# Hybrid layer on one core: the scan's broadcast rows issued by ACT in place of SP, with a new order of the main passes

## What is computed

```python
ssm = einsum('bti,si->bts', xc, W_x)          # 16 states, of each a row B and a row C
Bp, Cp = ssm[..., :16], ssm[..., 16:]
dt = softplus(einsum('bti,oi->bto', xc, W_dt) + b_dt)
def step(h, inp):
    x_t, b_t, c_t, dt_t = inp
    dA = exp(dt_t[..., None] * A)
    h = dA * h + dt_t[..., None] * b_t[:, None, :] * x_t[..., None]
    return h, einsum('bds,bs->bd', h, c_t)
```

## Time and profile before

| | |
|---|---|
| time, median of 3 runs | 3764.75 us (3763.28 to 3771.59) |
| the profiled execution | 3763.91 us, its span 3761.8 us |
| PE, ACT, DVE, POOL busy | 90%, 85%, 71%, 36% |
| DMA engines busy with the program's transfers | 47.4% |
| length of one pass of MAIN | 217.5 us |

### The profile page before, as it was taken

The page is one execution under the profiler, slowest core; times in us unless marked ns, Lnnn a source line. Parts: engine busy times, 40 slices in busy tenths (PEclk is TensorE's granted clock), DMA queues, the critical chain, the costliest instruction groups (busy, mean ns, idle before and its releaser), DMA issues. The chain is left out here.

```text
span 3761.8 us, 38380 instructions
## 1 busy us (share of the span) xinstructions
PE 3394.5 (90%) x11446; PEld 1446.9 (38%) x11446; DVE 2664.6 (71%) x3513; ACT 3199.0 (85%) x4034; POOL 1341.8 (36%) x758
## 2 busy tenths in 40 slices
PE   3896899999999999999999999999999999998847
PEld 1231334434343444434344443434344443434424
DVE  3537868687776868677686867778686877769582
ACT  2787899898999999899998989999998999886643
POOL 2112324344343434434342433424243443314251
PEclk9896899999999999999999999999999999999978
DMA  5324345455544545454454545454454645435332
GB/s 156 112 82 116 126 137 174 141 179 148 164 149 138 170 131 185 146 167 142 155 171 135 177 132 185 143 159 159 139 181 125 187 145 164 149 107 171 111 136 76
DMA packets 214847, 552.01 MB, mean 147 GB/s; under 512 B 25105, under 2 KB 96626, under 8 KB 214642
## 3 DMA queue, kind: packets, MB, share of 16 engines
q1 hardware_dynamic: 214642, 549.57, 47.4%
HBM read 488.65 MB, written 63.18 MB: 147 GB/s over the span
## 5 line engine op out<-in xcount | busy, mean ns | idle before, releaser
L785 PE MATMUL bank<-hF,wst 128*128 128x512 f32 x2304 | 1146.3, 619 | 29.7 <-ACT hF L887 15.2
L1332 POOL TENSOR_TENSOR yM<-yM,ws 128x1024 f32<-128x1024 f32 x240 | 630.6, 2628 | 1399.8 <-DVE ws L1231 1396.8
L1112 DVE TENSOR_TENSOR rPool<-bank,rPool 128x512 f32<-128x512 f32 x1024 | 700.5, 686 | 525.4 <-PE bank L713 411.5
L887 ACT ACTIVATE hF<-bank,cols 128x512 f32<-128x512 f32 x1152 | 771.6, 687 | 248.8 <-PE bank L774 233.6
L1025 ACT ACT_TABLE_LOAD x528 | 677.4, 1283 | 9.3
L887 ACT ACTIVATE rPool<-bank 128x512 f32<-128x512 f32 x1024 | 572.0, 597 | 92.5 <-PE bank L708 84.8
L772 PE MATMUL bank<-xnH,wst 128*128 128x512 f32 x1152 | 605.0, 525 | 30.3 <-ACT hF L887 18.3
L1224 DVE TENSOR_TENSOR_SCAN ws<-dAs,ws 128x1024 f32<-128x1024 f32 x256 | 598.7, 2345 | 7.2 <-ACT dAs L887 0.8
L785 PEld LDWEIGHTS bank<-hF,wst 128*128 128x128 f32 x2304 | 419.0, 193 | 464.2 <-issue 366.0
L713 PE MATMUL bank<-qpk,kpk 48*128 48x512 bf16 x1024 | 406.0, 398 | 97.8 <-DVE rPool L1112 93.6
L887 ACT ACTIVATE rPool<-rPool 128x2048 f32<-128x2048 f32 x256 | 490.5, 1916 | 2.1
(11 more groups left out here) (157 smaller groups left out, 2951.6 us busy)
## 6 DMA issues: line engine op xcount, KB each, us to landing
wst<-wscr SPq DMA_DIRECT2D x288, 768.0 KB, 5.9
bc<-bcscr SPq DMA_DIRECT2D x256, 512.0 KB, 4.6
cB<-gscr SPq DMA_DIRECT2D x256, 256.0 KB, 4.7
qscr<-parts SPq DMA_DIRECT2D x192, 128.0 KB, 2.4
kscr<-parts SPq DMA_DIRECT2D x192, 128.0 KB, 2.1
kpk<-kscr SPq DMA_DIRECT2D x128, 192.0 KB, 5.3
qpk<-qscr SPq DMA_DIRECT2D x128, 192.0 KB, 5.7
wscr<-wst SPq DMA_DIRECT2D x9, 512.0 KB, 5.5
```

What stands on the lines that cost most here:

```text
L785: pe.matmul(ps[FFN][:, :], w2, hF[:, (NCH * f + q) % HSLOTS, :], start=(c == 0), stop=(c == FC - 1)).then_inc(s_dn, 1)
L887: return nc.scalar.activation(out_, in_, fn, **kw)
L1112: v.tensor_tensor(rP[:, slot, c, :], ps[num_bank(b, s)][:, :], rP[:, slot, c, :], ALU.mult).then_inc(s_mul, 1)
L1332: g.tensor_tensor(yM[:, :, :], yM[:, :, :], ws[:, s % 3, :, :], ALU.add).then_inc(s_ya, 1)
```

## The change

`bc` leaves SP's order and enters ACT's. The code of the step stays the same apart from SP's `settled`, an increment of a semaphore that nobody waits for. In SECOND and LAST the orders of PE, DVE and POOL stay as they were, and ACT's is the old one with the `bc` steps put in; in MAIN the orders of all five engines are new. The number of steps of every kind stays the same on PE, DVE and POOL, and on ACT but for `bc`.

```diff
@@ SP, scan @@
                     sp.dma_start(bcscr[m].rearrange("s u t -> (s u) t"), rowBC[:, :]).then_inc(s_bcst, 16)
-                elif name == "bc":
-                    sp.wait_ge(s_bcst, floor(16 * (m + 1)))
-                    settled(sp)
-                    sp.wait_ge(s_hc, floor(NS * m + s - 1))
-                    settled(sp)
-                    src = bcscr[m][s:s + 1].rearrange("s u t -> s (u t)").broadcast_to([P, 2 * 512])
-                    sp.dma_start(bc[:, s % 2, :, :].rearrange("p u t -> p (u t)"), src).then_inc(s_bc[s % 2], 16)
@@ ACT @@
+            def rows_in(m, s):
+                act.wait_ge(s_bcst, floor(16 * (m + 1)))
+                act.wait_ge(s_hc, floor(NS * m + s - 1))
+                src = bcscr[m][s:s + 1].rearrange("s u t -> s (u t)").broadcast_to([P, 2 * 512])
+                nc.scalar.dma_start(bc[:, s % 2, :, :].rearrange("p u t -> p (u t)"), src).then_inc(s_bc[s % 2], 16)
+
...
-                    if kind == "M":
+                    if kind in ("M", "N") and name == "bc":
+                        rows_in(i - 1 if kind == "M" else i - 2, n)
+                    elif kind == "M":
                         scan(i - 1, name, n)
-                    if kind == "N":
+                    elif kind == "N":
                         decay(i - 2, n)
@@ MAIN, ACT: one line of the table, as an example @@
-    T.gelu H.gelu*2 T.log A.ln*4 N.decay A.ex T.gelu H.gelu*2 F.mean H.gelu*6 T.log A.ln N.decay A.ln*2 F.var A.ln*2
+    T.gelu H.gelu*2 T.log A.ln*2 N.decay N.bc A.ln*2 A.ex T.gelu H.gelu*2 N.bc F.mean H.gelu*6 T.log A.ln*2
```

More of the change, by code:

```diff
@@ L90 @@
     "SP": """
-    P.in F.w*3 F.rows F.gate F.w*2 F.gate*3 F.w F.gate F.w*3 F.gate*3 A.load M.rows M.bc*2 P.pk*2 A.load M.bc*2
-    P.pk*2 P.ahead M.bc*3 P.ahead
+    P.in F.w*3 F.rows F.gate F.w*2 F.gate*3 F.w F.gate F.w*3 F.gate*3 A.load M.rows P.pk*2 A.load P.pk*2 P.ahead*2
 """,
@@ L132 @@
 """,
     "PE": """
[L134 to L147, removed]
+    H.down*3 A.den*2 H.up A.den*2 A.num H.up H.down A.v F.mean H.down A.num H.down H.up*2 A.num H.up*4 A.num A.den*2
@@ L148 @@
+    A.num A.den*2 G.down*2 A.num*2 A.av A.num G.up*2 G.down*2 G.up*3 A.den*2 A.num*2 A.den A.num G.down A.av G.up
+    A.num G.down*2 G.up*2 A.num G.down A.den A.num A.den G.up A.num A.den*3 G.down A.num G.down A.den*2 G.up A.den
+    A.num A.av A.num*2 G.down*2 A.num*2 G.up*2 A.num*2 A.av*2 G.up*2 A.close
 """,
     "ACT": """
-    T.gelu H.gelu*2 T.log A.ln*4 N.decay A.ex T.gelu H.gelu*2 F.mean H.gelu*6 T.log A.ln N.decay A.ln*2 F.var A.ln*2
-    A.ex N.decay T.gelu H.gelu*2 T.log A.ln F.router N.decay T.gelu F.gelu*4 T.log A.ln*2 H.close P.load A.ln*2 A.ex
@@ L152 @@
[L152 to L156, removed]
@@ new lines @@
+    H.close A.ln P.load A.ex N.bc A.ln*2 P.mean A.ln*2 P.var N.decay*2 T.gelu F.gelu N.bc F.gelu*5 T.log A.ln*2 A.ex
+    P.qk A.ln*2 N.bc P.qk A.ex N.decay N.bc T.gelu F.gelu*6 T.log A.ln*4 P.qk A.ex N.decay A.ln*5 N.bc A.ex N.decay
+    T.gelu F.gelu*8 T.log A.ln*2 P.cast P.qk T.gelu F.gelu P.cast F.gelu*2 T.log A.ln E.mean A.ex A.ln*3 E.var A.ln
+    T.gelu F.gelu*3 P.cast F.gelu*2 T.log A.ex A.ln*2 G.mean G.var T.gelu F.gelu*4 P.cast T.log A.ln*2 G.router
+    P.cast T.gelu G.gelu*5 M.mean T.log M.var A.ex M.xp A.ln*2 M.xp T.gelu G.gelu*2 M.xp G.gelu*2 T.silu M.silu M.xp
@@ L170 @@
+    E.var E.gate F.part G.mean A.mul*2 F.part G.var A.mul G.router G.route F.part G.turn M.mean A.mul M.var A.mul*2
+    M.conv*8 A.mul*6 G.part A.mul M.dt M.dbx*2 M.scan M.hc A.mul G.part A.mul M.scan A.mul*2 M.dbx M.scan M.hc
+    G.part M.hc A.mul*4 M.dbx*2 A.mul M.scan A.mul*2 G.part A.mul M.scan M.hc A.mul*3 M.hc A.mul*2 G.part A.mul*3
+    M.dbx*2 M.scan*2 A.close M.hc*2
 """,
     "POOL": """
-    H.add N.acc*2 H.add*3 N.acc*5 F.add P.rope F.add N.acc*2 P.rest F.add*2 P.rest*2 P.rope P.rest F.add*3 M.take
```

66 lines of the change are left out of this document (37 added, 29 removed).

## The result

The changed kernel takes 3922.19 us (median of 4 runs, 3912.44 to 3923.45) where the kernel before takes 3768.17 on the same chip. The ratio is 1.0409, 95% interval 1.039 to 1.0428. It is 4.1% slower; the forecast was 0.4% slower, and the range ended at 3826 us. The profiled run took 3912.44 us, its span is 3910.4 us, 148.6 longer than that of before.

A forecast was written before the change was run, and what follows sets the result against it. The prediction took the PE-ACT round, with DVE third, to bound the kernel, not one engine. 13 x (0 + 0.5 - 0.3 + 0.7) = 11.7 us plus 3 for the end, on 3763.91, gave about 3778 us; range 3718 to 3826.

The forecast's parts named there:

- Issuing on ACT: ACT's queue: 256 `bc` issues of 0.32 us are paid beside running activations; nothing taken, 82 us the upper end.
- Waiting on ACT: ACT's sequencer, held until `hc` is ready, queues later instructions late: 0.5 us a pass taken, 1.8 at most.
- Given back by the transfers: DVE's waits for `bc` and PE's for expert weights shrink with a freer SP queue: -0.3 us a pass.
- The new order of PE: PE in MAIN: adjacent `A.num` pairs go from 2 to 7, costing 0.7 us a pass of a possible 4.3.
- the 10.8 us that it waits inside the runs: ACT's waits for `up` in a pass of MAIN, 139.9 us in 13 passes, would not shrink much.
- The end: LAST: `bc` issued late by ACT delays the finish by 0 to 6.7 us; 3 taken.
- The expectation of under 15: Sign in LAST: DVE's wait for `bc`, 14.7 us before, stays under 15 us.
- ACT paying in full: Rival: ACT's queue cannot hide issues and waits; 3830 us, ends 3800 and 3869, chance 0.07.
- The better order: Rival: the new MAIN order shortens PE's waits at the score products; 3735 us, chance 0.34.
- no change: Rival: issues and transfers are hidden and the new order equals the old; 3764 us, 3757 to 3771, chance 0.23.
- PE's wait at L713's counterpart grows from 3.6 us a pass: Sign in MAIN: PE waits longer for the numerators' bank at a score product than 3.6 us a pass.

The follow-up runs named there:

- issues_on_act: Kernel before, SP still issuing `bc`, plus 256 small transfers issued by ACT without a real wait: 3773.44 us, ratio 1.0032.
- waits_on_act: Kernel before, SP still issuing `bc`, with ACT only waiting for the same semaphores where it would issue `bc`: 3781.64 us, ratio 1.0050.
- sp_new_order: Kernel before, SP still issuing `bc`, with MAIN's new order on all five engines: 3919.73 us, ratio 1.0412.
- pairs_old: Kernel before, SP issuing `bc`, only PE's MAIN order edited to have the new order's adjacent `A.num` pairs: ratio 1.0128.
- the halves: Kernel before, SP issuing `bc`, MAIN's new order only up to `G.mean`: ratio 1.0259; only from there: 1.0472; only from behind `M.mean`: 1.0200.
- new_unpaired: sp_new_order with PE's adjacent `A.num` pairs parted down to two: ratio 1.0321 to the kernel before.
- run 14: Not a follow-up run: the words belong to the sentence that MAIN is run 14 times in the kernel, so no change or time of its own.
- act_old_order: Kernel before with `bc` issued by ACT, but MAIN's old order kept on every engine: 3809.96 us, ratio 1.0138.

## Why the prediction was wrong

- **Issuing on ACT, taken as nothing.** Right in mechanism. 256 issues cost 12 us by issues_on_act, not 82, and in the new order nothing that can be seen. Of the 84 us that ACT's issues last in the changed kernel, 74 lie beside running activations or table loads.
- **Waiting on ACT, 13 x 0.5 = 6.5 us.** Too small in the old order: 19 us (waits_on_act, 12 to 26) against a bound of 23. By which path they come is open, since PE stood still no longer there. In the new order, for which the term was meant, waits and issues together cost nothing that can be measured.
- **Given back by the transfers, -0.3 a pass.** The waits went the other way. DVE waits 28.0 us for rows in place of 5.9, PE for weights 2.8 in place of 1.4. Against sp_new_order the freer SP did serve the weights earlier (2.8 us for 7.2), but the rows, at their places on ACT, came later (28.0 us for none), and neither shows in the time.
- **The new order of PE, +0.7 a pass.** This is the step that failed. Measured: 145 us in 13 passes, 11.2 a pass, with the rows still issued by SP. The argument for a sixth of the pairs' price was that they "lie in a stretch where PE is hardly idle", from which it took them to be covered. It is the other way round: where PE is hardly idle, nothing covers a new wait. At full price the pairs would have been 4.3 us; pairs_old measured 3.6. The other 7 us or so had no term at all. The prediction asked of the new order only what it did to pairs, and not what else it moved on PE; the halves and new_unpaired (8.8 us a pass with two pairs, as before) show that this was the larger part. Nor had it a term for matmuls that take longer, 3.9 us of PE's busy time a pass. MAIN is also run 14 times and not 13, which by the prediction's own terms is 0.9 us.
- **"ACT's order has the same table loads and runs of `gelu`, so the 10.8 us that it waits inside the runs have no reason to shrink much."** They grew: 139.9 to 237.2 us, since ACT waits for PE's `up`. ACT's idle time in a pass, foreseen to grow by 1 us, went from 18.3 to 28.1. What matters is how one order lies to the other, and the sameness of one says nothing.
- **The end, +3.** Right in size: DVE's wait for rows in LAST rose from 14.7 to 19.6 us, 4.9 more, and the part behind MAIN grew by 5.5. The expectation of under 15 was missed.
- **Rivals.** ACT paying in full is refuted by issues_on_act, and with real transfers by act_old_order, 50 us in all and not 105. ACT's busy time, 200.19 us a pass for 199.18, which was to show it, can't: issues aren't counted in it. The prediction had said that a pass of 221 us or more would mean this rival; the pass is 228.3, and it means the order. A rule that reads one number for one cause was too short. The better order and no change are refuted by sp_new_order. The range left out a worse order altogether, though its other side, a better order by 29 us, was priced.
- **"PE's wait at L713's counterpart grows from 3.6 us a pass":** it did, to 8.2.

What stays open: which moved steps make the 7 to 9 us a pass that are not pairs. Most of them arise before `G.mean`, where the new order has only one pair more: 7.7 - 1.2 = 6.5 us there, against 5.5 behind `M.mean` with four pairs more, which at 3.6 / 5 = 0.7 us each leave about 5.8 and 2.6. No experiment went to single steps there.

## What to carry to other kernels

When two engines hand work to and fro below a microsecond, a rewritten order can be the largest part of a change, and not a side effect of it. Test it apart from the change, and price each new back-to-back use of a single buffer in full where the waiting engine has no slack. An engine that computes nothing is a good place for a transfer that must wait for a buffer, however long it stands there; on a computing engine the issue is nearly free, and the wait in front of it is not, and a place a few instructions too early can cost more than one that is too late.

## What the runs showed of the hardware

- A transfer issued by ACT takes 0.326 us on its queue, where SP took 0.320. 256 small ones of 0.33 us, issued by ACT with no wait, made the kernel only 12 us longer, some 0.05 us each.
- A wait on ACT ahead of such an issue holds up what stands behind it: ACT stood for 5.73 us with a table load behind a `bc` whose buffer wasn't free.
- Three waits of 0.8 us close to each other were followed by 4 us of PE at a granted clock of 0.57, in all 13 passes; three such waits some 3.3 us apart were not, in any. Of the 140 us, PE stands still for 90, and 50 are the same matmuls taking longer, about 44 of them at the lower clock.
